# A quantised feed-forward block takes over its layer norm, and part of its work changes engine

## The reference

```python
BLOCK = 16
_GRID = [0.0, 0.5, 1.0, 1.5, 2.0, 3.0, 4.0, 6.0]
_MID = [0.25, 0.75, 1.25, 1.75, 2.5, 3.5, 5.0]

def fp4_quant_dequant(x):            # blocks of 16 along the last axis
    scale = jnp.max(jnp.abs(xb), axis=-1, keepdims=True) / 6.0
    scale = jnp.maximum(scale, 1e-12)
    xn = xb / scale
    idx = jnp.searchsorted(_MID, jnp.abs(xn))
    return _GRID[idx] * jnp.sign(xn) * scale

def _L2_ffn_ref(x, w_gate, w_up, w_down):      # 128 -> 352 -> 128
    # fp4_linear(x, w): einsum('bsk,nk->bsn') of both sides quantised
    h = jax.nn.silu(fp4_linear(x, w_gate)) * fp4_linear(x, w_up)
    return fp4_linear(h, w_down)

x = x + _L2_ffn_ref(_layernorm(x, axis=-1), L2_ffn_w_gate, L2_ffn_w_up, L2_ffn_w_down)
```

## Time and profile before

| what | value |
|---|---|
| median of three executions | 4883.48 us (4876.37 to 4888.40) |
| the profiled execution | 4899.99 us |
| its span in the trace | 4898.1 us |
| busy over the span: PE, DVE, ACT, POOL | 62%, 59%, 33%, 44% |
| granted TensorE clock over the span | 0.772 of full speed |
| norm stage of the last feed-forward | 25.2 us (4686.3 to 4711.5) |
| its quantised stage | 177.6 us (4711.5 to 4889.1) |

### The profile page before, as it was taken

The page is one execution under the profiler, slowest core; times in us unless marked ns, Lnnn a source line. Parts: engine busy times, 40 slices in busy tenths (PEclk is TensorE's granted clock), DMA queues, the critical chain, the costliest instruction groups (busy, mean ns, idle before and its releaser), DMA issues. The chain is left out here.

```text
span 4898.1 us, 68375 instructions
## 1 busy us (share of the span) xinstructions
PE 3060.9 (62%) x23645; PEld 1853.7 (38%) x23645; DVE 2911.2 (59%) x6195; ACT 1599.0 (33%) x2718; POOL 2139.8 (44%) x2749
## 2 busy tenths in 40 slices
PE   5767266665294226666667756477756687656856
PEld 4567011111194115545523324333334233334534
DVE  4534476664434783343356658667659566487768
ACT  2212046554021102332225532145522245412611
POOL 6553420100433104303335438534477445477676
PEclk9778578786597556896869977689967699776877
DMA  5022222110131002101122200122100222000000
GB/s 145 36 77 66 53 73 68 51 49 1 51 91 49 0 7 69 46 0 41 46 78 60 74 2 1 27 79 62 46 1 0 63 70 64 18 1 1 1 0 18
DMA packets 218170, 206.27 MB, mean 42 GB/s; under 512 B 50439, under 2 KB 195015, under 8 KB 217080
## 3 DMA queue, kind: packets, MB, share of 16 engines
q1 hardware_dynamic: 205560, 176.85, 13.2%
q0 software_dynamic: 12288, 25.19, 1.7%
...
...
## 5 line engine op out<-in xcount | busy, mean ns | idle before, releaser
L829 DVE TENSOR_REDUCE l0b_negm<-l0b_ps_s 128x2 f32<-128x1024 f32 x256 | 302.7, 1220 | 173.4 <-PE l0b_ps_s L626 173.2
L708 ACT ACTIVATE l0b_E<-l0b_ps_t 128x1024 f32<-128x1024 f32 x256 | 262.0, 1024 | 233.1 <-PE l0b_ps_t L608 232.9
L829 DVE TENSOR_REDUCE l3a_negm<-l3a_ps_s 128x2 f32<-128x256 f32 (+3 forms) x256 | 199.1, 818 | 105.8 <-PE l3a_ps_s L632 105.4
L829 DVE TENSOR_REDUCE l2a_negm<-l2a_ps_s 128x2 f32<-128x256 f32 (+3 forms) x256 | 199.0, 818 | 100.9 <-PE l2a_ps_s L632 100.5
L829 DVE TENSOR_REDUCE l2b_negm<-l2b_ps_s 128x2 f32<-128x256 f32 (+3 forms) x256 | 199.0, 818 | 88.8 <-PE l2b_ps_s L632 88.4
L708 ACT ACTIVATE l3a_E<-l3a_ps_t 128x768 f32<-128x768 f32 (+1 forms) x192 | 169.3, 882 | 188.3 <-PE l3a_ps_t L608 188.1
L708 ACT ACTIVATE l2a_E<-l2a_ps_t 128x768 f32<-128x768 f32 (+1 forms) x192 | 169.4, 882 | 184.8 <-PE l2a_ps_t L608 184.5
L708 ACT ACTIVATE l2b_E<-l2b_ps_t 128x768 f32<-128x768 f32 (+1 forms) x192 | 169.4, 882 | 152.3 <-PE l2b_ps_t L608 152.1
L775 POOL TENSOR_SCALAR_AFFINE_SELECT l3a_E<-l3a_E 128x256 f32<-128x256 f32 x256 | 101.5, 409 | 231.3 <-ACT l3a_E L708 229.1
L775 POOL TENSOR_SCALAR_AFFINE_SELECT l2a_E<-l2a_E 128x256 f32<-128x256 f32 x256 | 101.5, 409 | 228.8 <-ACT l2a_E L708 226.3
L775 POOL TENSOR_SCALAR_AFFINE_SELECT l2b_E<-l2b_E 128x256 f32<-128x256 f32 x256 | 101.4, 410 | 220.8 <-ACT l2b_E L708 220.7
...
## 6 DMA issues: line engine op xcount, KB each, us to landing
...
```

The costliest lines, as they stand in the source:

```text
L708: act.activation(probs(n % 3, c, 0)[:, 2 * p:2 * p + 2, :], ps_t[:, :, 0:width[c]], ACT.Exp, scale=scale).then_inc(probs_ready.sem, 1)
L829: e = dve.tensor_reduce(negm[:, qt, :, j], ps_s[n % 2][:, :, off:off + keys[qt]], AX.X, ALU.max, negate=True)
```

## The change

It has five parts. The first three are in the quantised stage, the fourth removes a stage, and the last does not touch the order of any work.

1. The layer norm moves into the quantised stage. DVE takes the statistics of batches 0 to 2 at the start of the stage; for batches 3 to 7 ACT takes them between its other work (`row_sums`: a sum and a sum of squared deviations for each tile). POOL raises to -0.5 (`roots`), DVE makes the shift (`row_shift`) and the variance (`row_variance`), and ACT normalises four tiles at a time (`normalise`), with scale and bias from SBUF.
2. Of POOL's nine operations on a unit the squaring goes to ACT (`squares`), and the first scaling (`scale_x`) is issued one unit ahead, into one of two buffers. Block scales are taken three batches ahead into three buffers.
3. The residual is added on PE: a product of the identity and X opens each accumulation, and ACT copies the sum to X (`read_out`); DVE's add is gone.
4. The separate norm stages of `l2fa`, `l2fb`, `l3fa` and `l3fb` are gone, with their transposes and copies to XNT.
5. The attention stages share one set of semaphores, with running counts, where each had its own.

```diff
                     place_max(2 * b + 1)
                 if g == 2 and l in (0, 4) and 0 <= b + 2 < B:
...
+        x_scale = [sb(f"x_scale{u}", [P, 2 * NX]) for u in range(3)]
+        x_inv = [sb(f"x_inv{u}", [P, 2 * NX]) for u in range(3)]
+        x_v = [sb(f"x_v{u}", [P, NX, BLOCK]) for u in range(2)]
+        x_square = [sb(f"x_square{u}", [P, NX, BLOCK]) for u in range(2)]
...
+            def roots(b):
+                pool.wait_ge(row_stats_ready.sem, row_stats_ready.upto(b + 1))
+                pool.tensor_tensor(rstd[:, tiles(b)], var[:, tiles(b)], core.minus_half[:, 0:TB],
+                                   ALU.pow).then_inc(row_rstd_ready.sem, 1)
+
+            def half(u):
+                return slice(u % 2 * NX, (u % 2 + 1) * NX)
+
+            def scale_x(u):
+                pool.wait_ge(x_inv_ready.sem, x_inv_ready.upto(u // 2 + 1))
+                if u >= 2:
+                    pool.wait_ge(xq_ready.sem, xq_ready.upto(u - 1))
+                pool.tensor_tensor(x_v[u % 2][:, :, :], blocks(x_tiles(u)), wide(x_inv[u // 2 % 3][:, half(u)], NX),
+                                   ALU.mult).then_inc(scaled_ready.sem, 1)
...
             def quantize_x(u):
+                v, square = x_v[u % 2][:, :, :], x_square[u % 2][:, :, :]
                 if u >= 1:
                     pool.wait_ge(xq_ready.sem, xq_ready.upto(u))
                 if u >= 2:
                     pool.wait_ge(xqT_in_psum.sem, xqT_in_psum.upto(u - 1))
-                pool.wait_ge(x_inv_ready.sem, x_inv_ready.upto(u // 2 + 1))
-                half = slice(u % 2 * NX, (u % 2 + 1) * NX)
-                ch.link(pool.tensor_tensor(x_v[:, :, :], blocks(x_tiles(u)), wide(x_inv[u // 2 % 2][:, half], NX), ALU.mult))
-                ch.link(pool.tensor_tensor(x_square[:, :, :], x_v[:, :, :], x_v[:, :, :], ALU.mult))
-                pool.tensor_scalar(x_power[:, :, :], x_square[:, :, :], 4.0, MAGIC, ALU.is_ge, ALU.mult)
-                ch.link(pool.tensor_scalar(x_square[:, :, :], x_square[:, :, :], 16.0, 2.0 * MAGIC, ALU.is_ge, ALU.mult))
-                ch.link(pool.tensor_tensor(x_power[:, :, :], x_power[:, :, :], x_square[:, :, :], ALU.add))
+                pool.wait_ge(squares_ready.sem, squares_ready.upto(u + 1))
+                pool.tensor_scalar(x_power[:, :, :], square, 4.0, MAGIC, ALU.is_ge, ALU.mult)
+                ch.link(pool.tensor_scalar(square, square, 16.0, 2.0 * MAGIC, ALU.is_ge, ALU.mult))
+                ch.link(pool.tensor_tensor(x_power[:, :, :], x_power[:, :, :], square, ALU.add))
                 ch.link(pool.tensor_scalar(x_power[:, :, :], x_power[:, :, :], MAGIC, None, ALU.add))
-                ch.link(pool.tensor_tensor(x_v[:, :, :], x_v[:, :, :], x_power[:, :, :], ALU.add))
-                ch.link(pool.tensor_tensor(x_v[:, :, :], x_v[:, :, :], x_power[:, :, :], ALU.subtract))
-                pool.tensor_tensor(blocks(xq[u % 2][:, :, :]), x_v[:, :, :], wide(x_scale[u // 2 % 2][:, half], NX),
+                ch.link(pool.tensor_tensor(v, v, x_power[:, :, :], ALU.add))
+                ch.link(pool.tensor_tensor(v, v, x_power[:, :, :], ALU.subtract))
+                pool.tensor_tensor(blocks(xq[u % 2][:, :, :]), v, wide(x_scale[u // 2 % 3][:, half(u)], NX),
                                    ALU.mult).then_inc(xq_ready.sem, 1)
 
+            roots(0)
+            roots(1)
+            scale_x(0)
+            roots(2)
+            scale_x(1)
             for u in range(ALL):
                 quantize_x(u)
+                if u % 2 == 0 and u >= 2 and u // 2 + 2 < B:
+                    roots(u // 2 + 2)
+                if u + 2 < ALL:
+                    scale_x(u + 2)
             pool_step.per = ch.k
 
...
+            def row_statistics(b):
+                for n in range(b * TB, (b + 1) * TB):
+                    e = dve.bn_stats(stats[:, n, :], core.X[:, n, :])
+                ch.link(e)
+                for n in range(b * TB, (b + 1) * TB):
+                    e = dve.bn_aggr(mv[:, n, :], stats[:, n, :])
+                ch.link(e)
+                dve.tensor_scalar(minus_mean[:, tiles(b)], mv[:, tiles(b), 0], -1.0, None, ALU.mult)
+                dve.tensor_scalar(var[:, tiles(b)], mv[:, tiles(b), 1], LN_EPS, None, ALU.add).then_inc(row_stats_ready.sem, 1)
+
+            def row_variance(b):
+                dve.wait_ge(row_mean_ready.sem, row_mean_ready.upto(4 * (b - 2)))
+                dve.tensor_scalar(var[:, tiles(b)], deviation[:, tiles(b)], 1.0 / D, LN_EPS, ALU.mult,
+                                  ALU.add).then_inc(row_stats_ready.sem, 1)
+
+            def row_shift(b):
+                dve.wait_ge(row_rstd_ready.sem, row_rstd_ready.upto(b + 1))
+                dve.tensor_tensor(shift[:, tiles(b)], minus_mean[:, tiles(b)], rstd[:, tiles(b)],
+                                  ALU.mult).then_inc(row_bias_ready.sem, 1)
+
             def scales_x(b):
 
-                sc, i = x_scale[b % 2][:, :], x_inv[b % 2][:, :]
-                if b >= 2:
-                    dve.wait_ge(xq_ready.sem, xq_ready.upto(2 * (b - 1)))
+                dve.wait_ge(row_norm_ready.sem, row_norm_ready.upto(b + 1))
+                sc, i = x_scale[b % 3][:, :], x_inv[b % 3][:, :]
+                if b >= 3:
+                    dve.wait_ge(xq_ready.sem, xq_ready.upto(2 * (b - 2)))
                 ch.link(dve.tensor_reduce(sc, blocks(core.XN[:, b * TB:(b + 1) * TB, :]), AX.X, ALU.max, apply_absolute_value=True))
...
-            def add(u):
-                x = core.X[:, u * T2:(u + 1) * T2, :]
-                dve.wait_ge(out_ready.sem, out_ready.upto(u + 1))
-                dve.tensor_tensor(x, x, ps_o[:, :, :], ALU.add).then_inc(out_read.sem, 1)
-
+            row_statistics(0)
+            row_statistics(1)
+            row_shift(0)
+            row_shift(1)
             scales_x(0)
+            row_statistics(2)
             scales_x(1)
+            row_shift(2)
+            row_variance(3)
             for u in range(ALL):
                 for t in range(T2):
                     multiply(u, t)
-                if u % 2 == 1 and u // 2 + 2 < B:
-                    scales_x(u // 2 + 2)
+                if u == 0:
+                    scales_x(2)
+                if u % 2 == 1 and (u + 5) // 2 < B:
+                    scales_x((u + 5) // 2)
                 quantize_h(u)
-                if u >= 1:
-                    add(u - 1)
-            add(ALL - 1)
+                if u % 2 == 0 and u // 2 + 3 < B:
+                    row_shift(u // 2 + 3)
+                if u % 2 == 1 and (u + 7) // 2 < B:
+                    row_variance((u + 7) // 2)
             dve_step.per = ch.k
...
                 for t in range(T2):
+                    pe.matmul(ps_o[:, t, :], core.identf[:, :], core.X[:, u * T2 + t, :], start=True, stop=False)
                     for c, (lo, hi) in enumerate(CHUNKS):
                         mm = pe.matmul(ps_o[:, t, :], hT[u % 2][0:hi - lo, c, t * P:(t + 1) * P], w_outT[0:hi - lo, c, :],
-                                       start=(c == 0), stop=(c == 2))
+                                       start=False, stop=(c == 2))
                 mm.then_inc(out_ready.sem, 1)
...
+            def read_out(u):
+                act.wait_ge(out_ready.sem, out_ready.upto(u + 1))
+                act.activation(core.X[:, u * T2:(u + 1) * T2, :], ps_o[:, :, :], ACT.Copy).then_inc(out_read.sem, 1)
+
+            def row_sums(b, pair):
+
+                n0 = b * TB + 2 * pair
+                for n in (n0, n0 + 1):
+                    e = act.activation(seen[:, n % TB, :], core.X[:, n, :], ACT.Copy, scale=-1.0 / D, accum_out=minus_mean[:, n:n + 1])
+                e.then_inc(row_mean_ready.sem, 1)
+                act.wait_ge(row_mean_ready.sem, row_mean_ready.upto(4 * (b - 3) + 2 * pair + 1))
+                for n in (n0, n0 + 1):
+                    e = act.activation(seen[:, n % TB, :], core.X[:, n, :], ACT.Square, bias=minus_mean[:, n:n + 1],
+                                       accum_out=deviation[:, n:n + 1])
+                e.then_inc(row_mean_ready.sem, 1)
+
+            def normalise(b):
+                act.wait_ge(row_bias_ready.sem, row_bias_ready.upto(b + 1))
+                for n in range(b * TB, (b + 1) * TB):
+                    e = act.activation(core.XN[:, n, :], core.X[:, n, :], ACT.Identity, bias=shift[:, n:n + 1], scale=rstd[:, n:n + 1])
+                e.then_inc(row_norm_ready.sem, 1)
+
+            def squares(u):
+                act.wait_ge(scaled_ready.sem, scaled_ready.upto(u + 1))
+                if u >= 2:
+                    act.wait_ge(xq_ready.sem, xq_ready.upto(u - 1))
+                act.activation(x_square[u % 2][:, :, :], x_v[u % 2][:, :, :], ACT.Square).then_inc(squares_ready.sem, 1)
+
+            normalise(0)
+            normalise(1)
+            row_sums(3, 0)
+            squares(0)
+            normalise(2)
+            squares(1)
+            row_sums(3, 1)
+            row_sums(4, 0)
             read_xT(0)
```

(17 more changed lines are left out.)

82 lines of the change are left out of this document (53 added, 29 removed).

## The result

| | before | after |
|---|---|---|
| median, us (11 runs each) | 4880.28 | 4869.73 |
| range, us | 4872.61 to 4889.85 | 4859.52 to 4886.09 |
| ratio after / before, with its 95% interval | | 0.9979 [0.9969, 0.9988] |
| span of the profiled execution, us | 4898.1 | 4869.9 |

The change makes the kernel 0.21% faster (0.12 to 0.31%), some 10 us of 4880. Forecast were 6 us more. The time lies inside the forecast's range, and on the other side of no change. All ratios are taken from executions in the chip's usual state; a single execution, 5363 us at a granted clock of 0.59 in the experiment on the semaphores, fell in a slower state and is left out.

A forecast was written before the change was run, and what follows sets the result against it. POOL and DVE, both without a gap in mid-stage and stretching each other, were taken as full, neither as the bound by its share. Per feed-forward 19.5 less, 18.1 and 3.0 more: 1.6 us, 6 for four, 4890 us; range 4842 to 4918.

The forecast's parts named there:

- The norm stage goes: Start of a feed-forward, first statistics to xq(2): 32.0 us against 51.5, a gain of 19.5 us.
- The squares make a ring: Quantised stage, xq(2) to xq(12): POOL's next unit waits for ACT's squares; five pairs 117.5 us against 99.4, 18.1 more.
- The end: After xq(12): three units at 10.6 us, 31.8 against 29.6, plus identity products in the tail; 3.0 us more, bounds 0 and 6.
- step 1: Start of a pair, from xq(u+2): PE transposes x and h, ACT copies both, then squares; done at 2.8 us.
- The ring: Chain through PE, ACT, DVE and POOL that sets a pair of units: 23.5 us in place of 19.9, bounds 20.7 and 24.7.
- Step 3: In a pair, ACT normalises four tiles of a later batch: 1.5 us taken, between 1.1 and 1.5, done at 4.3.
- Less stretch, faster: Rival: POOL and DVE take turns more than they overlap, a pair takes 22.0 us, kernel 4852 us; chance 0.22.
- The ring does not bind: Rival: POOL stays the bound at 19.6 us a pair, whole norm gained, kernel 4798 us; chance 0.05.
- TensorE joins the ring: Rival: output and input products delay the transposes of x(u+4); a pair takes 24.7 us, kernel 4920 us; chance 0.25.
- A lock for whole instructions: Rival: DVE and POOL exclude one another for whole instructions; 1.0 us more a pair, kernel 4910 us; chance 0.02.

## Why the forecast was wrong

The mechanism was the one forecast; one term of the sum was mis-sized. Means of the four feed-forwards, in us, read from the timelines as for l3fb above; the last column is after less before, and its sum is taken ahead of rounding:

| term | forecast | measured |
|---|---|---|
| to xq(2), "The norm stage goes" (l2fb and l3fb, where no weights stage lies in it) | -19.5 | -18.9 (51.48 to 32.58) |
| xq(2) to xq(12), "The squares make a ring" | +18.1 | +17.4 (99.16 to 116.59) |
| xq(12) to the end, "The end" | +3.0 | -0.5 (50.73 to 50.27) |
| sum | +1.6 | -1.9 |

Four times the sum is -8, beside the -10 of the medians. The forecast was +6. Of the 14 us between, the last term has 4 x 3.5; the first was forecast 0.6 too good and the second 0.7 too bad, which cancels.

**"The end" is the step that failed**: it was put at +3.0 us a stage, with 0 as its lower bound, and came at -0.5. Of the 3.5 us between, 1.4 are the way from xq over the squares to POOL's next start, 1.1 the seven operations of POOL, and 1.0 the tail behind xq(15).

*Its units.* "2.8, 0.1 and 7.7 make 10.6 a unit". Measured are 9.8 us in the mean of the twelve last units (three in each of four stages), and 9.5 to 10.1 singly. Units 14 and 15 of the last stage:

```profile
4823.15 1.37 POOL L2715 TENSOR_SCALAR l3fb_x_power<-l3fb_x_square 128x256 f32<-128x256 f32 x1 [1.66 <-ACT l3fb_x_square L2910]
4829.61 0.62 POOL L2721 TENSOR_TENSOR l3fb_xq<-l3fb_x_v,l3fb_x_scale 128x256 f32<-128x256 f32 x1
4832.96 1.08 POOL L2715 TENSOR_SCALAR l3fb_x_power<-l3fb_x_square 128x256 f32<-128x256 f32 x1 [2.73 <-ACT l3fb_x_square L2910]
4839.55 0.62 POOL L2721 TENSOR_TENSOR l3fb_xq<-l3fb_x_v,l3fb_x_scale 128x256 f32<-128x256 f32 x1
```

L2715 starts 2.4 and 2.7 us behind xq here (the xq ahead of these rows ends at 4820.72), 2.45 in the mean of twelve, for 2.8 and 0.1. The 2.8 rests on a row at the lower of TensorE's two clock levels. I had read step 1 from the earlier trace rows, and this is the granted clock (the third number from the end) of that stretch in the kernel before:

```profile
4797.10:4799.60 2.50, 1.97 (x8) 1.53 (x8) 2.40 (x7) 1.25 (x3) 2.25 (x4) 0.50 0.00 0
```

The changed kernel has the same step, from xq to the end of the squares, at either level. In l3fb the first pair and the one followed above:

```profile
4694.17:4696.97 2.80, 2.22 (x9) 1.78 (x10) 1.44 (x3) 1.55 (x5) 1.59 (x3) 0.50 0.00 0
4764.23:4766.47 2.24, 1.33 (x10) 1.09 (x11) 1.21 (x3) 1.70 (x6) 1.59 (x3) 1.00 0.03 7
```

At 0.50 it takes 2.80 us, as forecast, in the first pair of all four stages. At 0.82 to 1.00 it takes 2.24 or 2.25 us, in all of the twelve last units. For the pairs I had taken 0.2 off for a higher clock, for the end nothing.

The seven operations take 7.1 and 7.2 us in the rows above, 7.6 in the unit ahead of them and 7.33 in the mean of twelve, for 7.7. The ring makes DVE idle too, so POOL is stretched less than by a DVE without gaps: the change itself altered the duration that I took from rows of before. The kernel without rounding supports this by a dose: with DVE at work 20.2 us of 28.1 instead of 26.0 of 29.6, the same seven take 7.0, 6.5 and 6.5 us, and 6.7 in the mean of twelve. The second of these, from its timeline:

```profile
4760.41 1.28 POOL L2737 TENSOR_SCALAR l3fb_x_power<-l3fb_x_square 128x256 f32<-128x256 f32 x1 [1.54 <-ACT l3fb_x_square L2932]
4766.26 0.62 POOL L2743 TENSOR_TENSOR l3fb_xq<-l3fb_x_v,l3fb_x_scale 128x256 f32<-128x256 f32 x1
```

*Its tail.* I added 0.9 us for the identity product and forgot what goes from the same path; measured are 0.1 us less (21.1 to 20.9 in the mean). Two rows of the changed kernel's last products:

```profile
4856.41 0.79 PE L2844 MATMUL l3fb_ps_o<-X,identf 128*128 128x128 f32 x2 [0.53 <-ACT l3fb_hT L2882]
4860.18 0.38 ACT L2886 ACTIVATE X<-l3fb_ps_o 128x256 f32<-128x256 f32 x1 [3.81 <-PE l3fb_ps_o L2846]
```

The kernel before has this one in their place, and its addition starts at 4888.29:

```profile
4885.33 2.93 PE L2771 MATMUL l3fb_ps_o<-w_outT,l3fb_hT 128*128 128x128 f32 x12 [0.53 <-ACT l3fb_hT L2807]
```

From the first product to the result's read 3.8 us against 3.0: the identity product costs 0.8, as sized. But between xq(15) and hq(15) DVE no longer adds residuals. hq(15) comes 14.1 us behind xq(15) in three of four stages, before 15.2 to 15.6 in three of four. With the additions put back it is 15.0 in l2fa and the tail 20.5: in that stage the exchange is even. The other stages of that experiment, at the lower clock, have 16.2 to 17.3 and can't tell. I had struck the additions from the pairs, where they were on no path, and not from the end, where they were.

**The ring, step by step**, forecast and as read from the pair above: squares done 2.8 and 2.2, by the clock; normalise done 4.3 and 3.8; h reduced 5.7 and 5.4; hq(u+1) 13.5 and 13.1, by 7.7 of quantising where I had 7.8; POOL's start 16.0 and 15.6; pair 23.5 and 23.3. The wait of L2715 was forecast at 30 us or more in a stage and is 36 in all of l3fb, 30.1 of it in the pairs, in single waits of 0.8 to 5.2; L2758 and L2767 wait five times each, as forecast, 2.2 and 1.4 us in the mean. Step 3, four ACT operations with two operands from SBUF, takes 1.64 and not 1.5. That is the estimate of 1.6 by the Trainium skill ("ScalarE: Activation LUTs", section "What ACT_TABLE_LOAD costs"), so the rule, which I had set below my row, was the better guide.

**The rivals.** "Less stretch, faster" had the right sign, but it showed in the last units, at 0.4 us a unit, and not in the pairs, which came at 23.3 and not at 22.0; it is a third of what "The end" missed. "The ring does not bind" is refuted by three experiments: the squares early, on GpSimd and twice. "TensorE joins the ring" is refuted: the transposes of x in l3fb wait for xq all 16 times, and five pairs without the identity product are no shorter.

"A lock for whole instructions" was to lengthen the turns by 1.0 us a pair, and that price is refuted: the pairs did not get longer than forecast. Its mechanism is not, and I had read the earlier trace rows wrongly. These three rows lie behind the pair of units shown above:

```profile
4784.66 0.79 POOL L2719 TENSOR_TENSOR l3fb_x_v<-l3fb_x_v,l3fb_x_power 128x256 f32<-128x256 f32 x1
4784.90 1.30 DVE L2572 TENSOR_TENSOR l3fb_hq<-l3fb_v,l3fb_scale 128x704 f32<-128x704 f32 x1
4785.53 1.26 POOL L2720 TENSOR_TENSOR l3fb_x_v<-l3fb_x_v,l3fb_x_power 128x256 f32<-128x256 f32 x1
```

L2719 ends at 4785.45, L2572 0.75 us behind it, and L2720 0.59 us behind L2572. Each row begins while the other engine's still runs, and ends a fixed time behind that one's end. That is no single case. In the four feed-forwards of the kernels before and after, 238 rows of DVE's TENSOR_TENSOR on 128x704 are stretched to more than 1.15 us, and 226 of them end 0.74 or 0.75 us behind the end of an operation of POOL. POOL has 137 stretched TENSOR_TENSOR rows, and 133 end 0.58 or 0.59 us behind the end of one of DVE. Alone the two last 0.89 and at least 0.62 us. So a turn costs 0.74 and 0.58, the 1.33 of rows 5, and not 0.89 and 0.62, because the first 0.15 us or less of a row pass beside the other's turn. The rows of before had this price in them already. But for that start the trace agrees with the rule of the Trainium skill ("SBUF — State Buffer", section "SBUF: two separate sides"), by which the first comer keeps the shared ports for its whole instruction.

**The chances.** The forecast lay 6 us from no change, and the result 10 us on the other side, both inside what I had called no change, 14.7 us; the measurement could tell finer than that, 0.1%. Where two large terms cancel, the sign hangs on the small third one, and its lower bound of zero was already enough to turn it. The term came below even that bound, since no part of it stood for the additions that leave the tail.
